# Where the wide buffers of a fused attention and expert kernel begin in SBUF: moving operands 64 bytes past a multiple of 128, the others at a multiple of 128

## The chip, the cores and the metric

The kernel runs on one core of one Trainium2 chip. The metric is the device time of one execution in microseconds (us), the median of the runs. Matrix products run on TensorE, shown in the profile as PE (the products) and PEld (the loads of the stationary operand, which overlap the products); VectorE is DVE, ScalarE is ACT, GpSimd is POOL, and SyncE (SP) issues most of the DMAs.

## The reference, cut to what matters

The input x holds 64 sequences of 64 tokens with 256 features. The reference does two gated residual steps:

```
x = x + tanh(g_xattn) * cross_attention(layernorm(x), ctx, Wq, Wk, Wv, Wo, q_norm_w, k_norm_w, positions)
x = x + tanh(g_ffn)   * experts(layernorm(x), w_router, w_gate, w_up, w_down, ws_gate, ws_up, ws_down)
```

The attention has 16 query heads and 4 key and value heads of width 128. Queries and keys are normalised by their root mean square and turned by their positions, and keys and values are made from the context and the tokens together. The second step adds a shared gated network of inner width 352 to the weighted sum of the two chosen of 8 experts of inner width 176. All of it is float32.

## The kernel before, in words

The 4096 tokens are 32 tiles of 128 tokens (two sequences each). Each tile is worked through in 4 units, one for each key and value head, so there are 128 units. In a unit TensorE turns the keys and queries over to columns (`heads_T`, lines 1754 and 1758), adds the output projection of the unit two before (`project`, line 1795), makes scores (`scores`, 1769), turns over the probabilities of the unit before (`probs_T`, 1777), makes the queries of the unit two ahead (`queries`, 1697), applies the probabilities (`attend`, 1784) and makes the keys and values of the unit two ahead (`keys_values`, 1711). The order on each engine is written out by hand, and semaphores connect the engines.

A matmul is called as (output, stationary, moving). The stationary operand, 128 columns here, is loaded by a LDWEIGHTS of its own; the moving operand then streams past it. In the profile the names stand as output<-moving,stationary. Products with weights are done in three passes, since operands are split in a high and a low part of type float32r: high by high, high by low and low by high (`PASSES`). So a unit has 12 matmuls of 256 moving columns in `keys_values` and 12 in `project`, 6 of 512 columns in `queries`. The turnovers, `scores` and `attend` are plain float32. The first four units use unsplit float32 weights (`first_queries`, `first_keys_values`), and the first eight projections do (`first_project`).

After the attention, and partly laced into its end, come the shared network (32 tiles; `shared_half` at line 1828 with 352 moving columns, 12 matmuls a tile; `shared_down_part` at 1946 with 256 moving columns, 9 a tile) and 71 slots of 128 token rows for the experts (`slot_gate_up` at 2031 with 352 moving columns, 6 a slot; `slot_down` at 2048 to 2052 with 256 moving columns, 6 a slot).

SBUF is laid out by hand. `sb` takes the next free byte of a cursor, or of another cursor (`at`) where a buffer lies over one whose work is done. Before the change every buffer begins at a multiple of 64 bytes, and nothing more is asked. `parts` makes a high and a low buffer. What matters for the operands of TensorE:

```
kv_in = [parts(f"kv_in{p}", [P, DC, 4, S]) for p in range(2)]          # stationary in queries, keys_values
w_group = sb("w_group", [P, KVH, 2 * DC * (REP * HD + 2 * HD)], F32R)  # moving in both
wo_s = parts("wo", [P, H, D]);   aT = parts("aT", [P, REP, NB, S])     # moving, stationary in project
yS_both = [sb(f"yS{r}", ..., late_at if r < RING // 2 else ring_at) for r in range(RING)]
```

The shared network of tile t takes its stationary tokens from `yS` buffer t % 8; buffers 0 to 3 lie in one stretch of SBUF, buffers 4 to 7 over `kv_in`.

Of the kernel before, what the change touches and what calls it, by code (L numbers as in the profile page):

```python
# [19 lines left out]
F32 = mybir.dt.float32  # L20
F32R = mybir.dt.float32r
# [7 lines left out]
P = 128  # L29
B, S, D = 64, 64, 256  # L30
H, KVH, HD = 16, 4, 128
REP = H // KVH
NB = P // S
TILES = B * S // P
PAIRS = TILES // 2
DC = D // P
# [27 lines left out]
PI_BELOW = 3.1415925  # L64
PASSES = ((0, 0), (0, 1), (1, 0))
HI, LO = 0, 1


def need(eng, sem, count):
# [28 lines left out]
def flamingo(nc, x, ctxT, posx, posc, invf, g_xattn, g_ffn, q_w, k_w, wq, wkv, wo, wr, wg, wd, out):  # L98
    ctx = ExitStack()
    with ctx:  # L100

        cursor = [-(-nc.sbuf_base // 64) * 64]

        def sb(name, shape, dt, at=None):
            size = int(np.prod(shape[1:])) * mybir.dt.size(dt)
            where = cursor if at is None else at
            t = nc.alloc_sbuf_tensor_at(name, shape, dt, offset=where[0])
            where[0] += -(-size // 64) * 64
            return t

        def parts(name, shape, at=None):
            return [sb(f"{name}_{p}", shape, F32R, at) for p in ("hi", "lo")]


        ident = sb("ident", [P, P], F32)
        gates = sb("gates", [P, 2], F32)
        gates_raw = sb("gates_raw", [P, 2], F32)
        minus_half = sb("minus_half", [P, 8], F32)
# [17 lines left out]
        stage_at = list(cursor)  # L136
        GU, DN = 2 * FS + 2 * E * F, FC + E * EFC
        wg_at = list(cursor)
        wg_raw = sb("wg_raw", [P, DC, GU], F32)
        wd_at = list(cursor)  # L140
        wd_raw = sb("wd_raw", [P, DN, D], F32)

        wg_lo = sb("wg_lo", [P, DC, GU], F32R, wg_at)
        wd_lo = sb("wd_lo", [P, DN, D], F32R, wd_at)
        wq_raw = sb("wq_raw", [P, DC, H * HD], F32, stage_at)
        wkv_raw = sb("wkv_raw", [P, DC, KVH, 2 * HD], F32, stage_at)
        wo_raw = sb("wo_raw", [P, H, D], F32, stage_at)
        assert stage_at[0] <= cursor[0] and EFC == 2 and REST <= AGAIN
        stage_end = cursor[0]
        phase_at = list(cursor)  # L150

        w_group = sb("w_group", [P, KVH, 2 * DC * (REP * HD + 2 * HD)], F32R)
        back_at = [phase_at[0] + 4 * (KVH - 1) * 2 * DC * (REP * HD + 2 * HD)]
        back = [sb(f"back{n}", [P, P], F32, back_at) for n in range(3)]

# [11 lines left out]

        phase_end = cursor[0]
        wo_at = list(cursor)
        wo_s = parts("wo", [P, H, D])  # L170
        wo_end = cursor[0]
        turn_at = list(cursor)
        w_cos = sb("w_cos", [P, 3, 2, HALF], F32)
# [16 lines left out]
        x1_first = [sb(f"x1_first{n}", [P, 2, D], F32, at) for n, at in enumerate((x_in_at, ctx_raw_at))]  # L190
        ring_at = list(cursor)
        kv_in = [parts(f"kv_in{p}", [P, DC, 4, S]) for p in range(2)]
        ring_end = cursor[0]
        free_at = list(cursor)
# [9 lines left out]
        v_s = [sb(f"v{g}", [P, NB, HD], F32) for g in range(KVH)]  # L204
        early_at = list(cursor)
        qT = sb("qT", [P, NB, REP, S], F32)
        kT = sb("kT", [P, NB, P], F32)
        probs = sb("probs", [P, REP, P], F32)
        pT = sb("pT", [P, NB, REP * S], F32)
        aT = parts("aT", [P, REP, NB, S])  # L210
        early_end = cursor[0]
        neg_max = [sb(f"neg_max{p}", [P, REP], F32) for p in range(2)]
# [13 lines left out]
        pos_i = sb("pos_i", [P, 2 * TILES], I32, early_at)  # L226
        assert early_at[0] <= early_end and cursor[0] <= nc.sbuf_usable_end, (early_at, early_end, cursor)

        w2_hi_all = sb("w2_hi_all", [P, DC * GU + DN * D], F32R, phase_at)
        wg_s = [w2_hi_all[:, 0:DC * GU].rearrange("p (c n) -> p c n", c=DC), wg_lo]  # L230
        wd_s = [w2_hi_all[:, DC * GU:DC * GU + DN * D].rearrange("p (c n) -> p c n", c=DN), wd_lo]
        assert phase_at[0] <= phase_end and stage_at[0] <= stage_end, (phase_at, phase_end, stage_at, stage_end)
# [1919 lines left out]
```

How the kernel before makes its waits and increments, by code:

```python
def need(eng, sem, count):  # L69
    if not isinstance(count, int) or count > 0:
        eng.wait_ge(sem, count)
# [346 lines left out]
            def load_inputs(t, p):  # L419
                need(sp, x_normed, t - 1)
                sp.dma_start(x_in[p][:], x[bass.ds(t, 1), :, :].rearrange("a p n -> p (a n)")).then_inc(ld_x[p], 16)
                if isinstance(t, int) and t == 2:
                    sp.wait_ge(ctx_hi, 1)
                need(sp, ctx_lo, t - 2)
                sp.dma_start(ctx_raw[p][:], ctxT[bass.ds(t, 1), :, :, :].rearrange("a p c n -> p (a c) n")) \
                  .then_inc(ld_ctx[p], 16)
# [47 lines left out]
            def load_yS(t):  # L475
                i, r = divmod(t, RING // 2)
                if t >= RING:
                    sp.wait_ge(up_done, t - RING + 1)
                elif t >= RING // 2:
                    sp.wait_ge(q_done, 4 * TILES)
                    sp.wait_ge(kv_done, 4 * TILES)
                need(sp, ld_yS[r], 16 * i)
                sp.wait_ge(st_yT, 16 * (t + 1))
                sp.dma_start(yS_both[t % RING][:].rearrange("p a c n -> p (a c n)").bitcast(F32),
                             yT_dram[t, :, :]).then_inc(ld_yS[r], 16)
# [1 line left out]
            def load_x1_first():  # L487
                for p in range(2):
                    sp.wait_ge(st_x1[p], 16 * (PAIRS - 1))
                for n, (read, times) in enumerate(((x_normed, TILES), (ctx_lo, TILES - 1))):
                    sp.wait_ge(read, times)
# [1185 lines left out]
        @block.tensor  # L1678
        def _(pe):
            pe.wait_ge(consts_set, 9)
```

## Time and profile before

| | us |
|---|---|
| median of 3 runs | 1230.98 |
| lowest, highest | 1230.97, 1231.51 |
| the profiled execution, whole | 1232.5 |
| its span, first to last instruction | 1230.7 |
| PE busy | 1205.3 (98% of the span) |
| PEld busy | 1137.3 (92%) |
| DVE, POOL, ACT busy | 1008.7 (82%), 922.4 (75%), 884.9 (72%) |

The rows further down all come from the profiled execution. Its time is 1.5 us above the median, and its span 0.3 us below it. An end of a matmul in the rows is modelled: consecutive matmuls overlap in the record, so the rate at which TensorE works is read from the distance between two starts, or from the difference of mean durations of one shape.

### The profile page before, as it was taken

What the parts mean: (1) busy time and instruction counts of PE and PEld (TensorE: products, weight loads), DVE (VectorE), ACT (ScalarE), POOL (GpSimd) and SP (SyncE); (2) the same over time, 40 slices, a digit from 0 to 9 for tenths busy, and PEclk for the clock granted to TensorE, in tenths of its full rate; (3) what the DMA queues carried; (4) which work ended last, traced back from release to release, by engine and by line L of the source; (5) the groups of instructions that cost most, each with busy time, mean ns of one, the idle gap of its engine ahead of it and who ended that gap; (6) DMA issues with size and microseconds to landing.
All of it is one profiled execution on the core that took longest, in us unless ns stands there. A gap on an engine that the chain in (4) does not pass through costs nothing.

```text
span 1230.7 us, 31490 instructions
## 1 busy us (share of the span) xinstructions
PE 1205.3 (98%) x8781; PEld 1137.3 (92%) x8782; DVE 1008.7 (82%) x2992; ACT 884.9 (72%) x3754; POOL 922.4 (75%) x1124
## 2 busy tenths in 40 slices
PE   6899999999999999999999999999999999999998
PEld 3688999999999999999999999999999999999997
DVE  8788888888888888888888888888888677777443
ACT  7978777777777777777777777777777546666322
POOL 2778888888888888888888888888887425556654
PEclk9999999999999999999999999999999999999999
DMA  6634233322222222223333333222236536554575
GB/s 179 198 115 128 72 111 106 100 90 90 90 90 90 94 90 94 90 90 93 115 108 99 103 103 120 94 75 75 75 110 213 193 104 188 163 158 150 186 230 158
DMA packets 128792, 148.57 MB, mean 121 GB/s; under 512 B 13824, under 2 KB 108288, under 8 KB 127968
## 3 DMA queue, kind: packets, MB, share of 16 engines
q1 hardware_dynamic: 122256, 130.16, 34.8%
q0 software_dynamic: 6480, 17.77, 4.0%
q8 instruction: 22, 0.36, 0.1%
q14 instruction: 34, 0.28, 0.1%
HBM read 66.93 MB, written 80.76 MB: 120 GB/s over the span
## 4 chain that ended last, share of the span: by engine, by line
PE 94%; DVE 2%; ACT 2%; issue 1%; DMA 0%; SPq 0%; DVEq 0%
PE b_kv L1711 14%; PE b_q L1697 14%; PE b_o L1795 13%; PE b_sc L1769 9%; PE b_aT L1784 9%; PE b_pT L1777 5%; PE b_qT L1758 4%; PE b_q L2031 3%; PE b_kv L2031 3%; PE b_q L1828 2%; PE b_kT L1754 2%; PE b_kT L1828 2%; PE b_aT L1946 1%; PE b_aT L2048 1%; PE b_pT L2048 1%; PE b_o L1747 1%
## 5 line engine op out<-in xcount | busy, mean ns | idle before, releaser
L1711 PE MATMUL b_kv<-w_group,kv_in_hi 128*128 128x256 f32 x992 | 205.6, 305 | 0.0
L957 ACT ACTIVATE probs<-b_sc,neg_max 128x128 f32<-128x128 f32 x512 | 180.5, 372 | 0.1
L747 POOL TENSOR_TENSOR qk_r<-qk_me,minus_half 128x6 f32<-128x6 f32 x128 | 172.8, 1350 | 10.1
L751 POOL TENSOR_TENSOR q_rot<-q_rot,q_sin 128x512 f32<-128x512 f32 x128 | 164.4, 1284 | 6.7 <-DVE q_sin L1273 1.9
L1711 PEld LDWEIGHTS b_kv<-w_group,kv_in_hi 128*128 128x128 f32 x992 | 161.8, 190 | 6.7 <-issue 0.4
L1697 PE MATMUL b_q<-w_group,kv_in_hi 128*128 128x512 f32 x496 | 164.8, 413 | 0.0
L951 ACT ACTIVATE pT<-b_pT 128x512 f32<-128x512 f32 x128 | 76.7, 600 | 99.7 <-PE b_pT L1777 97.7
L1795 PE MATMUL b_o<-wo_hi,aT_hi 128*128 128x256 f32 x480 | 143.5, 299 | 0.1
L1769 PE MATMUL b_sc<-kT,qT 128*128 128x128 f32 x1024 | 135.9, 275 | 6.8 <-ACT qT L946 4.9
L754 POOL TENSOR_TENSOR q_rot<-q_rot,qk_r 128x512 f32<-128x512 f32 x128 | 133.7, 1044 | 10.0
L1711 PE MATMUL b_kv<-w_group,kv_in_lo 128*128 128x256 f32 x496 | 139.6, 282 | 0.0
L940 ACT ACTIVATE junk<-b_q 128x128 bf16<-128x128 f32 x512 | 133.9, 283 | 0.0
L1769 PEld LDWEIGHTS b_sc<-kT,qT 128*128 128x128 f32 x1024 | 124.7, 191 | 9.0 <-issue 8.1
L1795 PE MATMUL b_o<-wo_lo,aT_hi 128*128 128x256 f32 x480 | 133.0, 277 | 0.0
L1795 PE MATMUL b_o<-wo_hi,aT_lo 128*128 128x256 f32 x480 | 132.7, 276 | 0.0
L1784 PE MATMUL b_aT<-pT,v 128*128 128x256 f32 x512 | 131.4, 379 | 0.0
L745 POOL TENSOR_TENSOR qk_me<-qk_ms,eps_rms 128x6 f32<-128x6 f32 x128 | 32.2, 252 | 119.0 <-ACT junk L928 118.7
L1283 DVE TENSOR_REDUCE neg_max<-b_sc 128x4 f32<-128x512 f32 x128 | 88.3, 690 | 36.6 <-PE b_sc L1769 34.7
L1784 PEld LDWEIGHTS b_aT<-pT,v 128*128 128x128 f32 x512 | 96.5, 189 | 17.5 <-issue 0.5
L940 ACT ACTIVATION_READ_ACCUMULATOR junk<-b_q 128x1 f32 x512 | 111.2, 217 | 0.0
L957 ACT ACTIVATION_READ_ACCUMULATOR probs<-b_sc,neg_max 128x1 f32 x512 | 109.1, 213 | 0.0
L760 POOL TENSOR_TENSOR k_rot<-k_rot,k_sin 128x256 f32<-128x256 f32 x128 | 93.6, 731 | 11.4 <-DVE k_sin L1259 8.8
(309 smaller groups left out, 3937.5 us busy)
## 6 DMA issues: line engine op xcount, KB each, us to landing
xs_scratch<-zeros SPq DMA_DIRECT2D x34, 1032.0 KB, 6.3
s_in<-xs_scratch SPq DMA_DIRECT2D x71, 129.0 KB
yT_scratch<-yT SPq DMA_DIRECT2D x32, 256.0 KB
yS<-yT_scratch SPq DMA_DIRECT2D x32, 256.0 KB, 3.0
routed<-ys_scratch SPq DMA_DIRECT2D x32, 256.0 KB, 3.5
w_hi_all<-w_scratch SPq DMA_DIRECT2D x3, 1536.0 KB, 13.6
x_in<-in_x SPq DMA_DIRECT2D x32, 128.0 KB, 2.3
ctx_raw<-in_ctxT SPq DMA_DIRECT2D x32, 128.0 KB, 2.5
```

The costliest lines, as they stand in the source:

```text
L747: nc.gpsimd.tensor_tensor(qk_r[g % 2][:], qk_me[:], minus_half[:, 0:REP + NB], ALU.pow).then_inc(r_ready, 1)
L751: nc.gpsimd.tensor_tensor(q_rot[g % 2][:], q_rot[g % 2][:], q_sin[g % 2][:], ALU.add) \
L754: nc.gpsimd.tensor_tensor(q_rot[g % 2][:], q_rot[g % 2][:], qk_r[g % 2][:, 0:REP].unsqueeze(2).to_broadcast([P, REP, HD]), ALU.mult) \
L760: nc.gpsimd.tensor_tensor(k_rot[g % 2][:], k_rot[g % 2][:], k_sin[g % 2][:], ALU.add) \
L940: last = nc.scalar.activation(junk[:, h, :], b_q[:, h * HD:(h + 1) * HD], ACT.Square, scale=HD ** -0.5, accum_out=qk_ms[g % 2][:, h:h + 1])
L957: last = nc.scalar.activation(probs[:, j, :], b_sc[:, j * P:(j + 1) * P], ACT.Exp, bias=neg_max[g % 2][:, j:j + 1], accum_out=row_sum[g % ...
L1283: nc.vector.tensor_reduce(neg_max[g % 2][:], b_sc[:].rearrange("p (j n) -> p j n", j=REP), AX.X, ALU.max, negate=True).then_inc(max_ready, 1)
L1697: last = nc.tensor.matmul(b_q[:], kv_in[p][a][:, c, 1:3, :], wq_of(b, gg)[:, c, :], start=(c == 0 and (a, b) == PASSES[0]), stop=(c == DC ...
L1711: last = nc.tensor.matmul(b_kv[:, s * 2 * HD:(s + 1) * 2 * HD], kv_in[p][a][:, c, 2 * s:2 * s + 2, :], wkv_of(b, c)[:, g % KVH, :], start= ...
L1769: last = nc.tensor.matmul(b_sc[:, o:o + P], qT[:, s, 2 * j:2 * j + 2, :], kT[:, s, :], start=True, stop=True)
L1784: last = nc.tensor.matmul(b_aT[:, s * REP * S:(s + 1) * REP * S], v_s[g % KVH][:, s, :], pT[:, s, :], start=True, stop=True)
L1795: last = nc.tensor.matmul(b_o[:, 0:D], aT[a][:, h, :, :], wo_s[b][:, gg * REP + h, :], start=(gg == 0 and h == 0 and (a, b) == PASSES[0]), ...
```

## The change

No instruction is added, removed or moved. The layout alone changes. A buffer of 512 bytes or more in a partition now begins at a multiple of 128 bytes, or, if it is made with `moving=True`, 64 bytes past a multiple of 128. Buffers under 512 bytes still take the next multiple of 64.

```diff
+WIDE, LINE = 512, 128
-        def sb(name, shape, dt, at=None):
+        def sb(name, shape, dt, at=None, moving=False):
             size = int(np.prod(shape[1:])) * mybir.dt.size(dt)
             where = cursor if at is None else at
+            if size >= WIDE:
+                where[0] = -(-(where[0] - moving * LINE // 2) // LINE) * LINE + moving * LINE // 2
             t = nc.alloc_sbuf_tensor_at(name, shape, dt, offset=where[0])
-        wg_raw = sb("wg_raw", [P, DC, GU], F32)
+        wg_raw = sb("wg_raw", [P, DC, GU], F32, moving=True)
...
-        w_group = sb("w_group", [P, KVH, 2 * DC * (REP * HD + 2 * HD)], F32R)
+        w_group = sb("w_group", [P, KVH, 2 * DC * (REP * HD + 2 * HD)], F32R, moving=True)
...
-        wo_s = parts("wo", [P, H, D])
+        wo_s = parts("wo", [P, H, D], moving=True)
...
-            kT = sb("kT", [P, NB, P], F32)
+            kT = sb("kT", [P, NB, P], F32, moving=True)
...
-        w2_hi_all = sb("w2_hi_all", [P, DC * GU + DN * D], F32R, phase_at)
+        w2_hi_all = sb("w2_hi_all", [P, DC * GU + DN * D], F32R, phase_at, moving=True)
```

`wg_raw`, `wd_raw`, `wg_lo`, `wd_lo`, `wq_raw`, `wkv_raw` and `wo_raw` get `moving=True` as well. Worked through with the sizes in the code, the cursor arithmetic gives these starts, as the remainder by 128 (the slices that the matmuls take of these buffers begin at multiples of 128 from the start of the buffer):

| matmul | moving, before -> after | stationary, before -> after |
|---|---|---|
| `keys_values`, `queries` | w_group 64 -> 64 | kv_in 64 -> 0 |
| `project` | wo 64 -> 64 | aT 0 -> 0 |
| `scores` | kT 0 -> 64 | qT 0 -> 0 |
| `attend` | pT 0 -> 0 | v 0 -> 0 |
| `heads_T`, `probs_T` | ident 0 -> 0 | k_rot, q_rot, probs 0 -> 0 |
| other turnovers | ident 0 -> 0 | x_n, hid, s_hid 64 -> 0; s_in 64 or 0 -> 0 |
| `shared_half` | w_hi_all, wg_lo 64 -> 64 | yS0 to yS3 0 -> 0, yS4 to yS7 64 -> 0 |
| `shared_down_part`, `slot_down` | w_hi_all, wd_lo 64 -> 64 | hT, s_hT 64 -> 0 |
| `slot_gate_up` | w_hi_all, wg_lo 64 -> 64 | sT 64 -> 0 |
| `router` | wr 64 -> 64 | yT 0 -> 0 |

So of the moving operands only `kT` moves from one half of a 128-byte line to the other. Most of what moves is stationary operands and the buffers of DVE, ACT, POOL and the DMAs (`x_in`, `x_res`, `x1_out`, `ctx_raw`, the turning tables, `x1_most`, `routed`, `s_out`), which go from 64 to 0.

## Rows read from the trace of the kernel before

**Rows 1.** The page: busy time by engine, and the granted clock in 40 slices.

```profile
PE 1205.3 (98%) x8781; PEld 1137.3 (92%) x8782; DVE 1008.7 (82%) x2992; ACT 884.9 (72%) x3754; POOL 922.4 (75%) x1124
...
PEclk9999999999999999999999999999999999999999
```

**Rows 2.** The page: the chain that ended last, by engine.

```profile
PE 94%; DVE 2%; ACT 2%; issue 1%; DMA 0%; SPq 0%; DVEq 0%
```

**Rows 3.** Windows of the attention: busy us of each engine (instructions), clock, DMA.

```profile
500.00:900.00 400.00, 400.00 (x2994) 379.71 (x2994) 351.67 (x1005) 310.39 (x1439) 337.49 (x384) 1.00 0.30 94
```

**Rows 4.** Groups by line, PE: shapes xcount | busy us, mean ns | idle.

```profile
L1711 PE MATMUL b_kv<-w_group,kv_in_hi 128*128 128x256 f32 x992 | 205.6, 305 | 0.0
...
L1711 PE MATMUL b_kv<-w_group,kv_in_lo 128*128 128x256 f32 x496 | 139.6, 282 | 0.0
...
L1795 PE MATMUL b_o<-wo_lo,aT_hi 128*128 128x256 f32 x480 | 133.0, 277 | 0.0
L1795 PE MATMUL b_o<-wo_hi,aT_lo 128*128 128x256 f32 x480 | 132.7, 276 | 0.0
...
L2052 PE MATMUL b_aT<-wd_lo,s_hT_hi 128*128 x36 | 10.1, 282 | 0.0
...
L1946 PE MATMUL b_aT<-wd_lo,hT_hi 128*128 128x256 f32 x28 | 5.6, 283 | 0.0
```

**Rows 5.** Timeline of PE, one `keys_values` and the next `project`: start us, length us.

```profile
606.28 0.28 PE L1711 MATMUL b_kv<-w_group,kv_in_lo 128*128 128x256 f32 x1
...
607.36 0.28 PE L1711 MATMUL b_kv<-w_group,kv_in_lo 128*128 128x256 f32 x1
...
608.25 0.28 PE L1795 MATMUL b_o<-wo_lo,aT_hi 128*128 128x256 f32 x1
...
609.27 0.28 PE L1795 MATMUL b_o<-wo_lo,aT_hi 128*128 128x256 f32 x1
```

**Rows 6.** Groups by line, PE, from 1176.6 to 1179.9 us (tile 18, yS2).

```profile
L1828 PE MATMUL b_kT<-w_hi_all,yS 128*128 128x352 f32 x4 | 1.1, 323 | 0.0
...
L1828 PE MATMUL b_q<-wg_lo,yS 128*128 128x352 f32 x2 | 0.6, 322 | 0.0
```

**Rows 7.** The same from 1186.6 to 1189.9 us (tile 21, yS5).

```profile
L1828 PE MATMUL b_kT<-w_hi_all,yS 128*128 128x352 f32 x4 | 1.1, 320 | 0.0
...
L1828 PE MATMUL b_q<-wg_lo,yS 128*128 128x352 f32 x2 | 0.6, 324 | 0.0
```

**Rows 8.** Groups by line, PE: the 512-column matmuls of `queries`.

```profile
L1697 PE MATMUL b_q<-w_group,kv_in_hi 128*128 128x512 f32 x496 | 164.8, 413 | 0.0
...
L1697 PE MATMUL b_q<-w_group,kv_in_lo 128*128 128x512 f32 x248 | 97.6, 393 | 0.0
```

**Rows 9.** Timeline of PE and PEld around 559 us: scores, router, turnovers.

```profile
558.54 1.05 PE L1769 MATMUL b_sc<-kT,qT 128*128 128x128 f32 x8
559.35 0.59 PE L1920 MATMUL b_kT<-wr,yT 128*128 128x16 f32 x4
...
559.32 0.53 PEld L1920 LDWEIGHTS b_kT<-wr,yT 128*128 128x128 f32 x4
```

**Rows 10.** Groups by line: scores and two turnovers, PE.

```profile
L1769 PE MATMUL b_sc<-kT,qT 128*128 128x128 f32 x1024 | 135.9, 275 | 6.8 <-ACT qT L946 4.9 <-issue 1.9
...
L1758 PE MATMUL b_qT<-ident,q_rot 128*128 128x128 f32 x512 | 76.8, 273 | 0.0
...
L2040 PE MATMUL b_qT<-ident,s_hid 128*128 128x128 f32 x72 | 13.7, 272 | 0.1
```

**Rows 11.** Timelines of ACT and PE: the query copy and the scores, two units.

```profile
565.19 0.60 ACT L946 ACTIVATE qT<-b_qT 128x512 f32<-128x512 f32 x1
...
571.96 0.60 ACT L946 ACTIVATE qT<-b_qT 128x512 f32<-128x512 f32 x1
...
566.00 1.06 PE L1769 MATMUL b_sc<-kT,qT 128*128 128x128 f32 x8
...
573.14 1.05 PE L1769 MATMUL b_sc<-kT,qT 128*128 128x128 f32 x8
```

More of the change, by code:

```diff
@@ L109, in sb, with parts @@
             return t
-        def parts(name, shape, at=None):
-            return [sb(f"{name}_{p}", shape, F32R, at) for p in ("hi", "lo")]
+        def parts(name, shape, at=None, moving=False):
+            return [sb(f"{name}_{p}", shape, F32R, at, moving) for p in ("hi", "lo")]
         ident = sb("ident", [P, P], F32)
@@ L138, in flamingo @@
         wg_at = list(cursor)
-        wg_raw = sb("wg_raw", [P, DC, GU], F32)
+        wg_raw = sb("wg_raw", [P, DC, GU], F32, moving=True)
         wd_at = list(cursor)
[L141 to L147, printed above, removed]
+        wd_raw = sb("wd_raw", [P, DN, D], F32, moving=True)
+        wg_lo = sb("wg_lo", [P, DC, GU], F32R, wg_at, moving=True)
+        wd_lo = sb("wd_lo", [P, DN, D], F32R, wd_at, moving=True)
+        wq_raw = sb("wq_raw", [P, DC, H * HD], F32, stage_at, moving=True)
+        wkv_raw = sb("wkv_raw", [P, DC, KVH, 2 * HD], F32, stage_at, moving=True)
+        wo_raw = sb("wo_raw", [P, H, D], F32, stage_at, moving=True)
         assert stage_at[0] <= cursor[0] and EFC == 2 and REST <= AGAIN
```

## The prediction

> **What bounds the kernel now.** I read the page's busy shares and clock first, then the chain that ended last, then the windows by stage. TensorE is the bound: its products are busy for 98% of the span at an undisturbed clock of 2.4 GHz [rows 1], it holds 94% of the chain [rows 2], and from 500 to 900 us it is busy for all 400.00 us while DVE, POOL and ACT stand at 351.67, 337.49 and 310.39 [rows 3]. The DMA share there is 0.30. So whatever changes the time of a DVE, ACT, POOL or DMA step by some per cent lies beside PE and costs nothing (the cover is 48 us of idle time in 400 on DVE, the fullest of them; it would be gone only if DVE's steps grew by about 14%). What counts is the pace at which matmuls follow each other, and then the groups by line, where one shape stands with different operands, are the view to read.
>
> **What the same shape costs at different homes.** The matmuls of 256 float32r columns are the lesson. Where moving and stationary operand begin at the same remainder by 128 (64 and 64) the mean is 282 ns in `keys_values`, 282 in the expert down product and 283 in the shared one; where they differ (wo at 64, aT at 0) it is 276 and 277 in `project` [rows 4]. The timeline gives the same as a pace: the low-part matmul of `keys_values` comes every third matmul, from 606.28 to 607.36 us nine matmuls pass, 120 ns each; in `project` nine pass from 608.25 to 609.27 us, 113 ns each [rows 5]. The two differ in shape and passes in nothing that I can find, so I price the step from equal to different remainders at 6 ns for each 256-column matmul that follows another (the durations; the starts say 6.7).
>
> For this there is a rule that speaks against the change. The moving and the stationary operand are read through two ports that do not disturb each other, says the Trainium skill (TensorE: Matmul & The Clock Gate, Step-by-step: what each phase is for): "Loading the next tile's weights doesn't steal SBUF read bandwidth from the running matmul." By that rule no start of a buffer matters and the time stays at 1231; the 6 ns between rows of one shape are not explained by it, and I follow the rows.
>
> **Part by part.**
>
> Keys and values: kv_in goes from 64 to 0, w_group stays at 64, the relation of `project`. The two groups hold 992 + 496 = 1488 matmuls [rows 4], 124 groups of 12. The first of a group follows `attend` and is left out: 11 x 124 = 1364, by 6 ns = 8.2 us.
>
> Down products: s_hT and hT go from 64 to 0 against weights at 64. 71 slots x 6 matmuls, 5 of 6 counted: 355 x 6 ns = 2.1 us. 32 tiles x 9, 8 of 9 counted: 256 x 6 ns = 1.5 us. Their present 282 and 283 ns are those of `keys_values` [rows 4], so the same price is fair.
>
> 352 columns (`shared_half`, `slot_gate_up`): here the trace holds a trial of its own, because yS0 to yS3 are at 0 and yS4 to yS7 at 64 against weights at 64. Tile 18, on yS2, has 323 and 322 ns; tile 21, on yS5, has 320 and 324 [rows 6, 7]. The remainder is worth nothing here, or costs up to 3 ns when it differs. I take 0. Bounds: 71 x 6 + half of 32 x 12 = 618 matmuls that change their relation, from nothing to +3 ns, so 0 to +1.9 us.
>
> 512 columns (`queries`): 744 matmuls [rows 8], same buffers as keys and values, relation changed. No row has this shape with another relation. From below the price of 256 columns, 744 x 6 = -4.5 us; from above the worse row of 352 columns, 744 x 3 = +2.2 us. By width it is nearest to 352, where the load of the next operand ends well before the stream does (in 256 columns of float32r both take about as long, so that each load meets a matmul for its whole length). I take 0.
>
> Scores: kT goes from 0 to 64, qT stays at 0. Eight of them start and end in 1.05 us and one lasts 275 ns, so the pace is (1050 - 275) / 7 = 111 ns, where turnovers of the same width stand at 272 to 273 ns a piece against 275 [rows 9, 10]. Does that gap of 2 to 3 ns go? The router's matmuls stream only 16 columns, wr at 64 and yT at 0, so there is next to nothing to meet, and four of them still take 0.59 us with 256 ns of their own, again 111 ns a step, with loads just as dense [rows 9]. That is the pace of the loads themselves, and the scores already run at it. I take 0; the bound below is 3 ns x 896 followers = -2.7 us, above 0.
>
> Turnovers: s_hid at 64 and q_rot at 0, both against ident at 0, take 272 and 273 ns [rows 10]. So moving x_n, hid, s_hid and s_in to 0 costs nothing. `attend`, `project`, `router` and the first units keep their relation or are plain float32, and count as 0 (bounds 0, for lack of any row of theirs that changes).
>
> DVE, ACT, POOL, DMA: their buffers go from 64 to 0. The page does not tell these apart by buffer. I bound it by the idle share above and cost it at nothing.
>
> **What is late next.** A faster PE meets its own waits sooner. The place is the scores of the first unit of a tile: the copy of the queries ends at 565.19 + 0.60 = 565.79 us and the scores start at 566.00, 0.21 us later, against 0.58 us in the next unit (571.96 + 0.60 to 573.14) [rows 11]. Of the 0.21 us the load before the first matmul takes about 0.11 (one pace), so 0.1 us is spare, and `keys_values` just before, whose time ACT uses for its squares, shrinks by 11 x 6 = 66 ns. This just fits. For the tiles where it does not I add 0.5 us (32 tiles, 16 ns each).
>
> Sum: 8.2 + 2.1 + 1.5 = 11.8 us off, 0.5 us on, so 11.3 us less. The profiled execution took 1232.5 us whole and would take 1221.2; the median of the runs is 1.5 us lower, 1231.0, and becomes 1219.7. I say 1220.
>
> **The rivals.**
>
> (a) The wider matmuls and the scores gain as well. For: they read the same way. Against: the 352-column rows and the router's pace. Time: 1219.7 - 4.5 - 2.7 = 1212.5; with `queries` alone 1215.
>
> (b) ACT or DVE takes back a part. For: 0.1 us of room in one unit of a tile [rows 11], DVE at 88% in the attention [rows 3]. Against: half a microsecond of room in the next unit. If in half of the 124 units the 66 ns of `keys_values` turn into a wait, 4.1 us come back: about 1224.
>
> (c) Nothing happens: the rule above holds, and `project` is fast for another reason (its stationary operand lies elsewhere, or its place in the unit). For: the yS rows, where the relation makes no difference. Against: three separate 256-column products with equal remainders all at 282 to 283 ns, one with different at 276 to 277. Time: 1231.
>
> (d) Slower: different remainders are worse for wide moving operands, as one pair of the yS rows says (323 against 320), and the 256-column gain isn't there. Price: 3 ns on 744 + 618 = 1362 matmuls is 4.1 us, time 1235. It decides as soon as those 3 ns are real and `keys_values` gains less than 1 ns per matmul. Against it: the other pair, 322 against 324.
>
> **How the numbers follow.** Chances: forecast 0.50 (its own range 1217 to 1223), (a) 0.18, (b) 0.13, (c) 0.14, (d) 0.05. For this kernel 0.2%, about 2.5 us, is what a measurement can tell from no change. Forecast, (a) and (b) are faster by more than that: 0.81. (c) is within it: 0.14. (d) is slower: 0.05. The range goes from 1212, the whole of (a), to 1230, which takes in a small rest of the gain and leaves out (d) and most of (c).
>
> **What would show it.** In the groups by line of the changed kernel the L1711 low-part matmuls fall from 282 to 276 ns, and so do L2052 and L1946; L1697 stays near 393, L1828 and L2031 at 320 to 324, L1769 at 275. The PE window from 500 to 900 us stays full. PE's wait for ACT qT grows by tenths. If L1711 stays at 282 the forecast is wrong by (c); if it falls and the span doesn't follow, by (b); if L1697 or L1769 falls too, by (a).

## The result, and the profile after

The changed kernel takes 1234.88 us in the median of 8 runs (1234.39 to 1235.15), the kernel before 1231.01 us in the median of 8 runs beside them (1230.47 to 1231.66): ratio 1.0031, 95% interval 1.0020 to 1.0042. It is 3.9 us slower. The forecast was 1220, range 1212 to 1230, with 0.81 on faster. It was wrong in size and in sign.

The page of the changed kernel, busy time by engine and the chain that ended last, shows the same bound as [rows 1, 2]:

```profile
PE 1209.5 (98%) x8781; PEld 1140.4 (93%) x8782; DVE 1007.0 (82%) x2992; ACT 883.8 (72%) x3754; POOL 918.0 (74%) x1124
...
PE 94%; DVE 2%; ACT 2%; issue 1%; DMA 0%; SPq 0%; DVEq 0%
```

PE was busy for 1205.3 us and is for 1209.5, with the same 8781 instructions. Nothing new is waited for; the same products take longer. The windows (busy us and instructions of PE, granted clock, DMA share, GB/s) say in which stage, first of the changed kernel:

```profile
0.00:100.00 100.00, 86.25 (x450) 0.98 0.58 171
500.00:900.00 400.00, 400.00 (x2983) 1.00 0.30 95
900.00:1230.00 330.00, 325.94 (x2408) 1.00 0.55 173
```

PE is as full from 500 to 900 us as in [rows 3], but it gets through 2983 products where it got through 2994. The granted clock of the first 100 us reads 0.98 in this execution. It read 1.00 in the profiled execution of before, and it reads 0.98 or 1.00 in the layouts below with no tie to their time, so I don't count it as the layout's.

The groups by line of the changed kernel (its lines stand 3 further down), which answer to [rows 4, 8, 10]:

```profile
L1714 PE MATMUL b_kv<-w_group,kv_in_hi 128*128 128x256 f32 x992 | 203.9, 304 | 0.0
L1700 PE MATMUL b_q<-w_group,kv_in_hi 128*128 128x512 f32 x496 | 166.3, 416 | 0.0
L1714 PE MATMUL b_kv<-w_group,kv_in_lo 128*128 128x256 f32 x496 | 139.9, 282 | 0.0
L1772 PE MATMUL b_sc<-kT,qT 128*128 128x128 f32 x1024 | 136.1, 276 | 6.1 <-ACT qT L949 4.2 <-issue 1.9
L1798 PE MATMUL b_o<-wo_hi,aT_lo 128*128 128x256 f32 x480 | 134.9, 281 | 0.0
L1798 PE MATMUL b_o<-wo_lo,aT_hi 128*128 128x256 f32 x480 | 134.8, 281 | 0.0
L1700 PE MATMUL b_q<-w_group,kv_in_lo 128*128 128x512 f32 x248 | 97.6, 394 | 0.0
L1761 PE MATMUL b_qT<-ident,q_rot 128*128 128x128 f32 x512 | 76.7, 272 | 0.0
...
L2051 PE MATMUL b_aT<-wd_lo,s_hT_hi 128*128 x36 | 10.1, 280 | 0.0
L2055 PE MATMUL b_aT<-wd_lo,s_hT_hi 128*128 x36 | 10.0, 277 | 0.0
...
L1949 PE MATMUL b_aT<-wd_lo,hT_hi 128*128 128x256 f32 x28 | 5.6, 281 | 0.0
```

The row that was to fall, `keys_values` with kv_in_lo, stands at 282 as before. The rows that were to stay, `project`, rose from 277 and 276 to 281. `queries` rose from 413 to 416. The slots' down product fell from 282 to 277, the shared one from 283 to 281. The wait for ACT's qT is shorter, not longer (4.2 us against 4.9).

The timeline, start and length in us, one `keys_values` and the next `project` of the changed kernel, for [rows 5]:

```profile
594.41 0.28 PE L1714 MATMUL b_kv<-w_group,kv_in_lo 128*128 128x256 f32 x1
...
595.47 0.29 PE L1714 MATMUL b_kv<-w_group,kv_in_lo 128*128 128x256 f32 x1
...
596.37 0.28 PE L1798 MATMUL b_o<-wo_lo,aT_hi 128*128 128x256 f32 x1
...
597.43 0.28 PE L1798 MATMUL b_o<-wo_lo,aT_hi 128*128 128x256 f32 x1
```

Nine matmuls take 1.06 us in both, 118 ns each. Before, they took 1.08 and 1.02.

A mean over a group hides what happens, so I took from the trace, for each `project` and `keys_values`, the mean distance between the recorded ends of consecutive matmuls, the first two distances left out. I call it the pace of a group, and count it to the whole ns. Paces come in three bands: 113 to 115, 118, and 119 to 120 ns. Before, 118 of 120 `project` groups run at 113 or 114 and all 124 `keys_values` at 119. After, 114 of 120 `project` groups run at 118, and 122 of 124 `keys_values` at 118. Added up from end to end over the profiled executions, after less before:

| PE | matmuls | us |
|---|---|---|
| `project` | 1440 | +4.8 |
| `queries` | 744 | +1.8 |
| `keys_values` | 1488 | -1.2 |
| `slot_down` | 355 | -1.6 |
| `slot_gate_up` | 426 | -1.0 |
| `shared_down_part` | 288 | -0.2 |
| `scores` and the k turnovers, waits included | 1280 | -1.5 |
| first units (unsplit weights) | | +0.9 |
| span, 1230.7 to 1232.6 | | +1.9 |

The parts sum to 1.9 us, the growth of the span. The medians grew by 3.9; the profiled execution of before lay 1.5 above its median and that of after 0.5 below, so the table is true to about 2 us, and more than that in the first units. A unit in the steady stretch, where the granted clock is 1.00 in both, is free of this: it takes 7.284 us before and 7.324 after (the mean over whole tiles), 40 ns more, 5.0 us over 124 units.

### The profile page after: what moved, and what is told of

Read it like the earlier page. It is cut to its first block, busy times and chain, and to the rows that moved or that the text cites. A ratio compares the mean times of both kernels' runs of the same rounds, so it can differ in the third digit from the quotient of the medians.

```text
span 1232.6 us, 31490 instructions
## 1 busy us (share of the span) xinstructions
PE 1209.5 (98%) x8781; PEld 1140.4 (93%) x8782; DVE 1007.0 (82%) x2992; ACT 883.8 (72%) x3754; POOL 918.0 (74%) x1124
## 4 chain that ended last, share of the span: by engine, by line
PE 94%; DVE 2%; ACT 2%; issue 1%; DMA 0%; SPq 0%; DVEq 0%
PE b_q L1700 14%; PE b_kv L1714 14%; PE b_o L1798 14%; PE b_sc L1772 9%; PE b_aT L1787 9%; PE b_pT L1780 5%; PE b_qT L1761 4%; PE b_q L2034 3%; PE b_kv L2034 3%; PE b_q L1831 2%; PE b_kT L1757 2%; PE b_kT L1831 2%; PE b_aT L1949 1%; PE b_o L1750 1%; PE b_pT L2051 1%; PE b_aT L2051 1%
```

## The experiments

Theory after the result: a group of 256-column matmuls locks into one of a few paces, and which one depends on the buffers' starts modulo 256, not 128, and on how the group is entered. The rivals: `project` is slower because of its own stationary operand, aT, or because of another engine's reads and writes. The starts modulo 256:

| | kv_in | q_rot, k_rot | v, qT | kT | probs, pT, aT | w_group, wo | ident |
|---|---|---|---|---|---|---|---|
| before | 64 | 128 | 128 | 128 | 128 | 64 | 128 |
| after | 128 | 0 | 0 | 64 | 128 | 64 | 128 |

All variants of the kernel are made by one edit, bytes added ahead of a named buffer (what lies behind it moves along, by amounts chosen to leave the other starts as they were modulo 256):

```diff
         def sb(name, shape, dt, at=None):
             where = cursor if at is None else at
+            where[0] += PAD.get(name, 0)
```

Ratios are to the kernel before, run beside the variant on the same chip, with the 95% interval behind them. e1 and e5 are one execution each.

**e1: TensorE alone.** Groups of 12 matmuls as in `project`, each after 4 to 7 turnovers, with the stationary operand at 8 starts (out_a at 0 modulo 512, out_b at 64, and so on) and the moving one at 0 (L97) or 64 (L101).

```diff
+for rep in range(8):
+    for l in LETTERS:                       # stationary start 0, 64, 128, ... 448
+        turns(l, 4 + (rep + LETTERS.index(l)) % 4)
+        for a, b, h, o, f in blocks(256, 4):
+            nc.tensor.matmul(banks[l][:, 0:256], sta(l, a, h), mov("b", b, o, 256), **f)
```

> This kernel leaves out all of the reference's work. TensorE alone works: groups of 4 to 7 turnovers and then 12 float32r matmuls of 256 columns in the three-pass pattern (later 6 of 352 or 512), with the stationary operand starting 0, 64, ... 448 bytes past a multiple of 512 (out_a to out_h) and the moving one 0 or 64 past it; no other engine touches SBUF meanwhile. Own-address theory (the distance of the two operands sets the pace): groups with 256 columns fall in classes by letter, some at about 276 ns a matmul (pace 113) and some at 281 to 283 (118 to 120), the same in all eight repetitions. Entry theory (the moment at which the group begins picks one of a few paces): each letter shows both, changing with the number of turnovers ahead. Traffic theory (the other engines' reads and writes of SBUF cost the 5 ns): all groups at about 276 or less, whatever the letter. 352 columns 320 to 324 and 512 columns 390 to 396 for the first two theories, about 310 and 375 for the third.

Measured, the timeline (start, length of the group of 12), with the moving operand at 64: a stationary start of 128 behind 7 turnovers, one of 64, and one of 128 again, here behind the 4 turnovers of the third row.

```profile
94.77 1.62 PE L101 MATMUL out_c<-mov_all,sta_all 128*128 128x256 f32 x12
...
124.94 1.68 PE L101 MATMUL out_b<-mov_all,sta_all 128*128 128x256 f32 x12
...
126.46 0.60 PE L85 MATMUL out_c<-ident,source 128*128 128x128 f32 x4
126.81 1.67 PE L101 MATMUL out_c<-mov_all,sta_all 128*128 128x256 f32 x12
```

With the moving operand at 64: equal starts (64 modulo 256) give 119 ns in 16 of 16 groups. A stationary start of 128 modulo 256 gives 113.4 to 115.1 in 12 of 16 and 118.3 in 4. 0 modulo 256 gives 118 in 12 of 16 and 113.6 in 4. 192 modulo 256 gives 118 to 120. The four slow groups of 128 are those behind exactly 4 turnovers (the last two rows), the four fast ones of 0 those behind 6. Here starts that lie 256 apart agree with each other. 352 columns take 159 to 162 ns, 512 columns 231 to 233, by the start. So no other engine is needed, the halves of a 128-byte line are not enough to tell the cases apart, and one relation has two paces.

The other half of the run, with the moving operand at 0, says the same 64 bytes lower. A stationary start of 64 gives 114 to 115 ns in 10 of 16 groups and 118 in 6, starts of 0 and 128 give 118 to 120, and 192 gives 118. Both halves together: where the two starts have the same remainder by 128, no group is fast (0 of 64). With the stationary start 64 above the moving one modulo 256, 22 of 32 are fast, and with it 64 below, 4 of 32. Starts 256 apart are not alike in one case here: behind 5 turnovers a stationary start of 64 runs at 115 and one of 320 at 118.

**e2 and e4: aT moved by 256**, in the kernel before and in the changed one.

```diff
+        PAD = {'aT_hi': 256}
```

> The kernel before with aT (and all behind it) 256 bytes further on, still at a multiple of 128 but now 384 past a multiple of 512 as in the changed kernel, instead of 128. Own-address theory: project goes from 276 to 281 ns a matmul as in the changed kernel, 1440 matmuls by 4.5 ns, about 1236 us; everything else stays. Entry or traffic theory: project stays at 276 to 277 and the time at 1231.

> The changed kernel with aT 256 bytes further on, so that it is again 128 past a multiple of 512 as in the kernel before. Own-address theory: project goes back from 281 to 276 ns and the time from 1234.9 to about 1229. Entry theory: project stays mostly at 281, with a few groups of the 120 at 276 as now, and the time at about 1235.

e2: 0.9998 (0.9989 to 1.0008), `project` at 113. e4: 1.0036 (1.0022 to 1.0050), 114 of 120 `project` groups at 118. So the place of aT modulo 512 is not the cause, and aT has the same start modulo 256 before and after.

**e3: kv_in to 128 modulo 256**, in the kernel before; junk, s_in, sT and s_hT, which lie behind it, move with it as in the change.

```diff
+        PAD = {'kv_in0_hi': 64, 'q_rot0': 448}
```

> The kernel before with kv_in alone moved from 64 to 0 past a multiple of 128 (and junk, s_in, sT, s_hT, which lie behind it); aT, kT, qT keep their places modulo 512. Own-address theory: keys_values at 281 to 282 ns with hardly any followers at 120 ns but at 118 (as in the changed kernel), queries 1 to 2 ns slower, project stays at 276; time 1229 to 1231. Entry theory: project, which comes 6 turnovers after keys_values, goes to 281 although nothing of its own moved; time about 1235.

1.0007 (0.9998 to 1.0017). `keys_values` (46 groups at 114, 78 at 118) gains 3.1 us in the end-to-end sum, `queries` loses 2.1, `project` 1.1. Neither theory's number came: `project` goes slow in 21 of its 120 groups, not in all or none. So the part on which the forecast stood nets nothing, and it is not the part that costs 3.9 us.

**e5: one unit's PE sequence, nothing else.** The unit's 52 products on ready data, 6 times for each of 24 layouts, without any wait. It computes none of the kernel's output.

```diff
+LAYOUTS = [BEFORE, AFTER, E3, ..., of(E3, kr=256, qr=256), ..., of(E3, pT=0), ..., of(BEFORE, aT=0), ...]
+for home in LAYOUTS:
+    for _ in range(6):
+        unit(home)
```

> This kernel leaves out all of the reference's work but TensorE's own sequence of one attention unit (6 turnovers, 12 project, 4 scores, 4 turnovers, 6 queries, 2 attend, 12 keys_values), six times for each of 24 layouts, back to back, with no waits and with no other engine at work. The layouts are the starts modulo 512 of before, of after, of before with kv_in moved (E3) and 21 others with one or two buffers moved. Address theory (TensorE's own operands, their distance modulo 256 and the moment at which a group begins, set the pace): a unit of before lasts some 7.10 us, one of after 40 to 50 ns longer, with project at 113 in the first and 118 in the second, and keys_values at 119 and 118; E3 in between. Traffic theory (other engines' accesses cost the rest): before and after differ by under 10 ns a unit and all 256-column groups with different remainders run at 113.

| layout (starts modulo 256) | unit, us | `project` | `keys_values` |
|---|---|---|---|
| before | 7.033 | 113 | 119 |
| after | 7.037, 7.077 in turn | 113, 118 in turn | 118 |
| before, kv_in 128 (as e3) | 7.040 | 113 | 118 |
| the same, q_rot and k_rot 0 | 7.073 | 118 | 118 |
| the same as e3, v 0 | 7.033 | 113 | 118 |
| the same as e3, pT 0 | 7.007 | 113 | 115 |
| before, q_rot, k_rot, v, qT 0 | 7.040 | 114 | 119 |
| before, kT 64 | 7.033 | 113 | 119 |
| before, aT 0 | 7.080 | 118 | 119 |
| before, aT 64 | 7.087 | 119 | 119 |

Ten of the 24 are shown. The others stay between 7.026 and 7.047 us or repeat one of these, but for one that alternates as after does (kv_in and pT both at 0: 7.029 and 7.071).

The timeline of two units in a row, same code, same layout (that of after): L102 is `project`.

```profile
93.16 1.62 PE L102 MATMUL b_o<-every 128*128 128x256 f32 x12
...
100.19 1.66 PE L102 MATMUL b_o<-every 128*128 128x256 f32 x12
```

And with kv_in at 128: q_rot and k_rot at 0 (first row), then pT at 0 (`project`, and L122, `keys_values`).

```profile
431.05 1.66 PE L102 MATMUL b_o<-every 128*128 128x256 f32 x12
...
515.60 1.62 PE L102 MATMUL b_o<-every 128*128 128x256 f32 x12
...
520.46 1.73 PE L122 MATMUL b_kv<-every 128*128 128x256 f32 x12
```

`project` has the same two operands at the same starts in the first four lines of the table; what differs is what ran before it. Its own starts count too: with aT at 0 or 64 it runs at 118 or 119. The sequence gives 24 ns a unit on average for the change (7.057 against 7.033 us) where the kernel shows 40: right in sign and place, too small in size, and between what the two theories had said. What makes up the rest is open.

**e6: the changed kernel with the turned buffers back at 128 modulo 256** (q_rot, k_rot, v, qT; kT goes to 192).

```diff
+        PAD = {'q_rot0': 128, 'probs': 128}
```

> The changed kernel with q_rot, q_sin, k_rot, k_sin, v, qT, probs, pT and aT put back to 128 past a multiple of 256 as in the kernel before (all still at a multiple of 128, so the change's own rule is kept); kT and kv_in and the rest as changed. Entry theory, with the starts of the turned-over operands as what moves the entry: project goes back to 276 ns in most groups, keys_values is at 276 in a part of them, time 1231 to 1233 where before is 1234 on that chip (3 to 4 us under the changed kernel). If only the 64-byte half counts: no change against the changed kernel, project stays at 281.

0.9987 (0.9978 to 0.9997), 1229.26 us against 1230.92: everything that the change lost is back, and a little more. 93 of 120 `project` groups run at 113 or 114, 96 of 124 `keys_values` at 114.

**e7 and e8: single moves in the kernel before**: q_rot, k_rot, v, qT and kT to 0 modulo 256, and kT alone to 64.

```diff
+        PAD = {'q_rot0': 128, 'probs': 128}          # e7
+        PAD = {'kT': 64, 'probs': 448}               # e8
```

> The kernel before with q_rot, q_sin, k_rot, k_sin, v, qT and kT at 0 past a multiple of 256 instead of 128, all still at a multiple of 128; kv_in stays at 64. Entry theory with those starts as what moves the entry: project goes to 281 ns in many groups, up to 5 us slower. Entry theory with keys_values and queries as what moves the entry, or the 64-byte half alone: project stays at 276, time within 1 us of before.

> The kernel before with kT alone at 64 past a multiple of 128. All theories: scores stay at 275 ns a matmul, since the loads set their pace, time within 1 us of before. If scores do gain (272), 2.7 us less. Entry theory: project may lose part of its 276 ns if scores' end moves what follows; more than 2 us slower would say that kT is the buffer that counts.

e7: 1.0002 (0.9992 to 1.0012), `project` at 113 or 114 in 118 groups. e8: 0.9999 (0.9989 to 1.0009). The turned buffers by themselves cost nothing, where one of the theories had up to 5 us. So the loss is neither that of kv_in (e3) nor that of the turned buffers (e7) but of both together.

**e9: both together**: e3 with q_rot and k_rot at 0, in the kernel before.

```diff
+        PAD = {'kv_in0_hi': 64, 'q_rot0': 576, 'v0': 128}
```

> Kernel before with kv_in from 64 to 0 (mod 128) as in e3, and q_rot and k_rot moved from 128 to 0 modulo 256; nothing else of the change. Theory (project's pace is picked by what TensorE reads just ahead of it, the turned queries and keys, once kv_in has moved): project falls back from 113 to 118 ns per matmul in most groups, 4.5 ns x 11 x 120 = some 5 us, so a time 0.2 to 0.4% above before, near that of the changed kernel. Rival (project's loss comes from another buffer of the change, v, qT, kT or probs, or needs all of them): as e3, ratio 1.000 to 1.001, project at 113 in most groups.

1.0035 (1.0021 to 1.0048), `project` at 118 in 116 of 120 groups, +4.4 us in the end-to-end sum: the whole loss of the change. q_sin and k_sin, which lie between, moved too, but TensorE doesn't read them, and e5 shows the step with TensorE alone (7.073 against 7.040 us). Groups by line:

```profile
L1713 PE MATMUL b_kv<-w_group,kv_in_lo 128*128 128x256 f32 x496 | 139.8, 282 | 0.0
L1797 PE MATMUL b_o<-wo_lo,aT_hi 128*128 128x256 f32 x480 | 134.8, 281 | 0.0
L1797 PE MATMUL b_o<-wo_hi,aT_lo 128*128 128x256 f32 x480 | 134.8, 281 | 0.0
```

**e10: the changed kernel with q_rot and k_rot alone back at 128.**

```diff
+        PAD = {'q_rot0': 128, 'v0': 128}
```

> Changed kernel with q_rot and k_rot alone put back to 128 modulo 256; v, qT, kT, s_in, hidden and aT as changed. Theory (the turned queries and keys pick project's pace): project back at 113 to 114, the time at 0.999 to 1.001 of before, some 4 us under the changed kernel. Rival (v or qT picks it): project stays at 118 and the ratio at 1.003.

0.9997 (0.9988 to 1.0006); `project` at 113 or 114 in 119 groups, `keys_values` at 118 in all 124. The groups by line say the same:

```profile
L1716 PE MATMUL b_kv<-w_group,kv_in_lo 128*128 128x256 f32 x496 | 139.8, 282 | 0.0
L1800 PE MATMUL b_o<-wo_lo,aT_hi 128*128 128x256 f32 x480 | 133.1, 277 | 0.0
L1800 PE MATMUL b_o<-wo_hi,aT_lo 128*128 128x256 f32 x480 | 132.6, 276 | 0.0
```

Two buffers that neither `project` nor `keys_values` reads, the operands of the six turnovers ahead of `project`, decide 4 us. The rival, v or qT, falls. q_rot and k_rot were not moved one without the other, so it is open which of them does it.

**e11 and e12: pT at 0 modulo 256**, in the layout of e3 and in that of e6.

```diff
+        PAD = {'kv_in0_hi': 64, 'q_rot0': 448, 'pT': 128, 'aT_hi': 128}    # e11
+        PAD = {'q_rot0': 128, 'probs': 128, 'pT': 128, 'aT_hi': 128}       # e12
```

> Kernel before with kv_in from 64 to 0 as in e3 and pT moved from 128 to 0 modulo 256, nothing else. From the sequence without other engines (e5: keys_values at 115 against 118 with this pT, the unit 34 ns shorter than e3's): keys_values at 114 to 115 in most groups, which is 3.5 ns x 11 x 124 = 4.8 us less than e3, so 0.996 to 0.998 of before. Rival (the pace in the whole kernel is picked by the waits for ACT and DVE, not by the buffer read ahead): keys_values mixed as in e3, 46 of 124 groups fast, ratio about 1.0005.

> The layout of e6 (changed kernel, turned buffers, probs and aT at 128 modulo 256) with pT at 0 modulo 256. Theory: keys_values at 114 to 115 in all groups (96 of 124 in e6) and project at 113 in all (93 of 120 in e6): ratio 0.996 to 0.998. Rival (the two do not add, the room is used up by ACT's or DVE's waits or the other group falls to its slow pace): 0.9985 or above.

e11: 0.9983 (0.9974 to 0.9992), 1228.82 us against 1230.98; 111 of 124 `keys_values` groups at 113 to 115, against 46 in e3. So the pace came as expected, and the time a little short of the 0.996 to 0.998: `project` is at 118 in 13 groups. e12: 0.9980 (0.9971 to 0.9989), 1228.67 us, the upper edge of what was expected and 0.2% under the kernel before; e11 and e12 can't be told apart; 122 of 124 `keys_values` at 114 or 115, -5.7 us in the end-to-end sum. Its groups by line:

```profile
L1716 PE MATMUL b_kv<-w_group,kv_in_lo 128*128 128x256 f32 x496 | 137.6, 277 | 0.0
L1800 PE MATMUL b_o<-wo_lo,aT_hi 128*128 128x256 f32 x480 | 133.4, 278 | 0.0
L1800 PE MATMUL b_o<-wo_hi,aT_lo 128*128 128x256 f32 x480 | 132.9, 277 | 0.0
```

Now `keys_values` stands at 277 ns, where the forecast promised 276 for this row. Its 5.7 us are 4.2 ns for each of the 1364 matmuls that the forecast priced at 6. Against them stand `queries`, which keeps its loss of 2.1 us, and `project`, where 20 of 120 groups are at 118 (0.9 us).

## Why the prediction was wrong

**The bound**: right. PE is 98% busy before and after, no cover gave way, and PE's waits for the other engines did not grow. The term of 0.5 us for ACT's copy of the queries was not needed: that wait shrank by 0.7 us. Rival (b) was hardly put to the test, since `keys_values` did not shrink; where it shrank by 5.7 us (e12), the end-to-end sum of `scores` grew by 0.8.

**"`attend`, `project`, `router` ... keep their relation and count as 0"**: this is the step that turned a gain into a loss, and its bounds of 0 failed with it. `project` kept both starts, by 128 and by 256, and lost 4.8 us. e9 and e10 pin that on the start of q_rot and k_rot, read by the turnovers just before it, once kv_in has moved as well; e2 and e4 show that aT's place modulo 512 has no part in it. The bound was set "for lack of any row of theirs that changes". No row of before could show that, and a lack of rows is a reason for wide bounds.

**The price of 6 ns from equal to different remainders**: this is the step that cost the forecast most, 7.0 us in `keys_values`, and it is half right. Equal remainders do hold a group at 118 to 120 ns and never at 113 (e1, 64 of 64). Leaving that relation only permits the fast pace. The price was read from `project` in a layout in which 118 of its 120 groups were fast, and taken as a property of the pair. `keys_values` got 1.2 us where 8.2 stood, 0.9 ns a matmul in place of 6. With pT moved too it got 5.1 (e11) and 5.7 (e12). The shared down product got 0.2 us of 1.5. For the slots' down product the price nearly held: it has 5 matmuls a slot (355 in the trace of before), not 6, so that 71 x 4 x 6 ns = 1.7 us should have stood in place of 2.1, and 1.6 came.

**Remainders by 128**: too coarse. In the table by 128, q_rot and k_rot go from 0 to 0; by 256 they go from 128 to 0.

**512 columns**: taken at 0 with bounds of -4.5 to +2.2 us; it is +1.8, 2.4 ns a matmul, not far from the 3 ns of the upper bound, which the 352-column row gave. e3, e6, e9 to e12 show 1.9 to 2.2 us each time kv_in is at 128. **352 columns**: 0 taken, `slot_gate_up` gained 1.0 us and `shared_half` lost 0.1. **Scores**: kT's half does nothing (e8). So rival (a) falls.

**The rivals.** (c), that nothing happens, is refuted by the time and, for single buffers, by e9 against e3. Its own sign did come: the low-part row of `keys_values` stayed at 282 ns. So did half of its reason, that `project` is fast for its place in the unit as well. The other half was the rule of the two read ports (the Trainium skill, TensorE: Matmul & The Clock Gate, Step-by-step: what each phase is for). What the prediction drew from that rule, that no start of a buffer matters, does not hold: in e1 the same 256-column product, with TensorE alone at work, runs at 119 ns with both starts at 64 and at 113 to 115 in 12 of 16 groups with the stationary one at 128. Whether a load then takes reads from the running matmul, no run shows. (d), the slower side, named 1235, and 1234.9 came. Its condition was half met, since `keys_values` gained under 1 ns a matmul and `queries` did lose 2.4 ns. But the 352-column products gained 0.9 us in sum where (d) had them lose, and most of the loss is in `project`, which (d) did not name, so its number was right by luck. It had 0.05. With a price that rested on three rows of one layout, "the pace of one group is moved by its neighbours" should have been a rival of its own.

**What stays open.** How the pace is chosen. In the traces the first matmul of a `project` group ends 122 to 124 ns after the turnover before it where the group then runs at 113 (117 of 120 before) and 119 to 121 ns after where it runs at 118 (113 of 114 after); the group that enters 3 ns sooner pays 4.5 ns for each matmul. In e5 21 of 118 groups at 113 to 115 entered at 119 to 121, so the first distance alone doesn't tell the two apart. e5's alternate units and e1's count of turnovers fit that the moment of entry chooses, and that the starts act by shifting this moment. That is a reading of records, not shown: the records' ends are modelled, and no run shifted the entry alone. Nor is it known why the remainder by 256 says most, and not quite all, of it.

## What to carry to other kernels

When a product with ready operands is the bound, look at the distance between consecutive ends within each group, not at the mean duration: if it takes a few fixed values, the group locks into one of them, and a price read from one group is one of its values, not its cost. A layout change then has to be tried together with its neighbours, and e3, e7 and e9 show that single moves worth nothing can cost 0.35% as a pair. Ask for the remainder modulo 256, not 128, before saying that a buffer's place is unchanged, and treat a term "without a row" as unbounded rather than as zero.

## What the runs showed of the hardware that was not expected

- A 256-column float32r product with a load for each matmul has three paces, 113 to 115, 118 and 119 to 120 ns, at a granted clock of 1.00, without any other engine at work (e1, e5).
- With equal remainders by 128 no group of e1 is fast (0 of 64); with the stationary operand 64 bytes above the moving one modulo 256, 22 of 32 are, and which ones changes with the number of turnovers ahead.
- One sequence in one layout took 7.037 and 7.077 us in turn, for six units, twice in the run (e5). So the pace of `project` follows a fixed pattern there and isn't chance.
- The start of the operands of 128-column turnovers, whose own mean stayed at 272 to 273 ns, moved the pace of the group behind them by 4.5 ns a matmul (e9, e10), and the start of the moving operand of `attend` that of `keys_values` behind it by 3 to 4 ns (e11; in e5 from 118 to 115).
- Starts that differ by 256 bytes behaved alike for aT in the kernel (e2, e4) and, with the moving operand at 64, in e1; with it at 0, one case of e1 differs (115 against 118 ns).
